# Second attention: the maxima of a pair's last four units come off in VectorE, from a broadcast tile, and not in TensorE's sum

## What is computed

```python
h = _layernorm(x, ln1_g, ln1_b)
# _attention(h, h, ...), 16 heads of 64, D_ATTN = 1024:
q = (xq @ wq).reshape(B, S, N_HEADS, D_HEAD)
...
attn = jnp.einsum('bihd,bjhd->bhij', q, k) * scale
attn = jax.nn.softmax(attn, axis=-1)
out = jnp.einsum('bhij,bjhd->bihd', attn, v).reshape(B, S, D_ATTN)
return out @ wo + bo
```

## Time and profile before

| | us |
|---|---|
| median of 3 runs | 2147.8 (2146.59 to 2148.71) |
| the profiled execution, its own time | 2148.86 |
| span of its profile | 2147.1 |
| TensorE busy in the span | 2020.2 (94%) |
| VectorE busy | 1134.3 (53%) |
| ScalarE busy | 929.5 (43%) |
| GpSimd busy | 773.0 (36%) |
| the second attention, from its first unit to its end | about 802 to 1680 |

### The profile page before, as it was taken

How to read it: one execution, slowest core, us unless ns; L and a number is a source line. 1 busy time by engine, 2 the same in 40 slices (tenths; PEclk the granted TensorE clock), 3 DMA queues, 4 the chain that set the end, 5 groups by cost and what they waited for, 6 DMA issues and landing times. The chain is left out here.

```text
span 2147.1 us, 26642 instructions
## 1 busy us (share of the span) xinstructions
PE 2020.2 (94%) x10302; PEld 1201.3 (56%) x10302; DVE 1134.3 (53%) x2025; ACT 929.5 (43%) x1441; POOL 773.0 (36%) x563
## 2 busy tenths in 40 slices
PE   5989998898998989999999999999999999999997
PEld 3544444576676754444544445444543878676776
DVE  4677772635455457756555554555454333546453
ACT  3356666333334325555445554555356431222221
POOL 1222212112223126666546664666564010212121
PEclk9999999899999989999999999999999999999999
DMA  7734332000000020200000000000000340000000
GB/s 145 137 36 52 42 57 85 1 1 1 0 1 1 1 67 1 70 1 1 1 1 1 1 1 1 1 1 1 1 1 1 97 112 1 1 10 0 10 10 10
DMA packets 48044, 51.81 MB, mean 24 GB/s; under 512 B 14682, under 2 KB 38940, under 8 KB 47620
## 3 DMA queue, kind: packets, MB, share of 16 engines
q1 hardware_dynamic: 47924, 50.19, 11.3%
HBM read 41.24 MB, written 8.80 MB: 23 GB/s over the span
## 5 line engine op out<-in xcount | busy, mean ns | idle before, releaser
L1921 POOL TENSOR_TENSOR total<-total,pr 128x1024 f32<-128x1024 f32 x183 | 444.2, 2427 | 230.9 <-ACT pr L2131 214.2
L2131 ACT ACTIVATE pr<-sc 128x1024 f32<-128x1024 f32 x256 | 259.8, 1022 | 267.0 <-PE sc L1797 262.4
L1942 DVE TENSOR_REDUCE pmax<-ring 128x1 f32<-128x512 f32 x512 | 314.5, 684 | 98.3 <-PE ring L1745 98.3
L1797 PE MATMUL sc<-q_full,k_full 64*128 64x512 f32 x1024 | 294.9, 589 | 0.0
L1815 PE MATMUL o<-pr,v_pair 128*64 128x512 f32 x1024 | 247.7, 605 | 0.0
L1745 PE MATMUL ring<-k_round,q_round 64*128 64x512 f32 x512 | 214.0, 568 | 6.0 <-DVE k_round L1936 2.0
L645 ACT ACTIVATE probs<-s 128x512 f32<-128x512 f32 (+1 forms) x304 | 154.8, 581 | 95.8 <-PE s L360 95.1
L993 POOL TENSOR_TENSOR c_scores<-c_scores,c_total 128x1024 f32<-128x1024 f32 (+1 forms) x48 | 76.5, 1615 | 237.6 <-DVE c_total L942 237.6
L483 DVE TENSOR_REDUCE row_max<-s 128x1 f32<-128x1024 f32 (+3 forms) x128 | 125.0, 1019 | 59.1 <-PE s L346 58.7
L1745 PEld LDWEIGHTS ring<-k_round,q_round 64*128 64x128 f32 x512 | 78.5, 189 | 137.6 <-DVE pmax L1942 115.5
L1797 PEld LDWEIGHTS sc<-q_full,k_full 64*128 64x128 f32 x1024 | 128.9, 191 | 25.9 <-issue 16.8
(11 more groups left out here) (349 smaller groups left out, 3425.1 us busy)
## 6 DMA issues: line engine op xcount, KB each, us to landing
qk_dram<-qk_parts SPq DMA_DIRECT2D x32, 192.0 KB, 2.7
q_stack<-qk_dram SPq DMA_DIRECT2D x48, 128.0 KB
k_stack<-qk_dram SPq DMA_DIRECT2D x48, 128.0 KB
x<-in_x SPq DMA_DIRECT2D x4, 512.0 KB, 7.4
region<-in_L_xattn_mlp_w SPq DMA_DIRECT2D x2, 1024.0 KB, 7.9
region<-in_L_xattn_ff_w SPq DMA_DIRECT2D x1, 2048.0 KB, 18.6
out<-region SPq DMA_DIRECT2D x8, 256.0 KB, 2.2
region<-in_L_xattn_sa_wo SPq DMA_DIRECT2D x1, 1024.0 KB, 8.1
```

Source lines behind the costliest of these rows:

```text
L1797: ins = te.matmul(s2[at % 2][:, j], kf[n % 2][head[j], keys], qf[n % 2][head[j], halves[half]], start=False, stop=True)
L1921: pool.tensor_tensor(out=total[half][:], in0=other[:], in1=probs[at % KEPT][:], op=ALU.add).then_inc(sums, 1)
L1942: dve.tensor_reduce(part_max[:, j, t, half:half + 1], ring[bank_of_max(i)][:], AX.X, ALU.max).then_inc(s1_free, 1)
L2131: act.activation(probs[here % KEPT][:], s2[at % 2][:], ACT.Exp).then_inc(s2_free, 1)
```

## The change

For units 12 to 15 of every pair but the last (`shifted_later`), TensorE no longer adds the maxima; the two scores' matmuls start the sum. In their place `less(n, u)` in VectorE reads the PSUM tile and adds `spread`, a tile that holds the negated maxima of half 1 in fp32 on all partitions, and writes the result to the `probs` tile; ScalarE takes the exponential in that tile, in place. The PSUM tile is free when `less` is done (`bank_free`) and not when the exponential is. `spread` is filled by two more transfers for each pair on SP's queue: `top` as a whole to DRAM, and from there, broadcast, 128 x 4 KB. Both writes to DRAM are waited for before the shift is read back; the broadcast is issued behind the shift, once the pair before has done its last `less`.

In VectorE's order `less(n, 12)` stands ahead of `split(n + 1)`, and `less(n, 13)` behind it; `less` of unit 13 stands ahead of the `late` work and the additions to `x` of that unit. Besides, the output bias is loaded into a tile that exists already (`proj_brep`), and two pairs of semaphores become one each, without other instructions.

```diff
@@ tiles and semaphores
-        wo_w, wo_brep = e.wide, sb("wo_brep", [P, C])
+        wo_w, wo_brep = e.wide, e.proj_brep
...
+        spread = sb("spread", [P, 2, 512])
...
+        spread_in, less_made = sem("spread_in"), sem("less_made")
...
+        LESS = 12
+        shifted_later = lambda n, u: u >= LESS and n + 1 < PAIRS
+        less_count = lambda n, u: (U - LESS) * n + u - LESS + 1
...
+        def buffer_free(engine, here):
+
+            if here < KEPT:
+                return
+            engine.wait_ge(pv_made, here - KEPT + 1)
+            half, kt = divmod((here - KEPT) % U, 8)
+            engine.wait_ge(sums, 7 * (2 * ((here - KEPT) // U) + half) + (kt or 1))
@@ SP
                 sp.dma_start(e.top_dram[n % 2, :, 0:16].rearrange("s r q -> r s q"), top_parts[n % 2][:]
                              ).then_inc(top_out, 16)
-                sp.wait_ge(top_out, 16 * (n + 1))
+                sp.dma_start(e.top_whole[n % 2], top[:]).then_inc(top_out, 16)
+                sp.wait_ge(top_out, 32 * (n + 1))
...
+                if n + 1 < PAIRS:
+                    if n:
+                        sp.wait_ge(less_made, less_count(n - 1, U - 1))
+                    sp.dma_start(spread[:], e.top_whole[n % 2].rearrange("(j t) q -> j (t q)", j=2)[:, 512:T]
+                                 .partition_broadcast(P)).then_inc(spread_in, 16)
@@ TensorE
+            def bank_free(at):
+                if at < 2:
+                    return
+                what, n, u = turns[at - 2]
+                if what == "unit" and shifted_later(n, u):
+                    te.wait_ge(less_made, less_count(n, u))
+                else:
+                    te.wait_ge(s2_free, at - 1)
...
-                if at >= 2:
-                    te.wait_ge(s2_free, at - 1)
+                bank_free(at)
                 keys = slice(kt * P, (kt + 1) * P)
-                for j in two:
-                    te.matmul(s2[at % 2][:, j], picks[head[j]], shift[n % 2][head[j], halves[half]], start=True,
-                              stop=False)
+                late = shifted_later(n, u)
+                if not late:
+                    for j in two:
+                        te.matmul(s2[at % 2][:, j], picks[head[j]], shift[n % 2][head[j], halves[half]], start=True,
+                                  stop=False)
                 for j in two:
                     ins = te.matmul(s2[at % 2][:, j], kf[n % 2][head[j], keys], qf[n % 2][head[j], halves[half]],
-                                    start=False, stop=True)
+                                    start=late, stop=True)
@@ VectorE
+            def less(n, u):
+                here, at = U * n + u, order_of(n, u)
+                dve.wait_ge(s2_made, at + 1)
+                dve.wait_ge(spread_in, 16 * (n + 1))
+                buffer_free(dve, here)
+                dve.tensor_tensor(out=probs[here % KEPT][:], in0=s2[at % 2][:], in1=spread[:], op=ALU.add
+                                  ).then_inc(less_made, 1)
...
                     if u == TURNED_AT - 1:
                         divide(n, 0)
+                    if shifted_later(n, u):
+                        less(n, u)
                     if u == TURNED_AT and n + 1 < PAIRS:
                         split(n + 1)
                     late(n, u)
@@ ScalarE
+                    if shifted_later(n, u):
+                        act.wait_ge(less_made, less_count(n, u))
+                        act.activation(probs[here % KEPT][:], probs[here % KEPT][:], ACT.Exp).then_inc(s2_free, 1)
```

More of the change, by code:

```diff
@@ L1638, in part_attention2 @@
         cand_less, cand_gated, mixed, power_set = (sem(n) for n in ("cand_less", "cand_gated", "mixed_late", "power_set2"))
[L1639 to L1642, removed]
+        n6_stats_made, n6_moments_made, n6_rstd_steps, n6_h_made, finished = (
+            sem(f"n6_{n}") for n in ("stats_made", "moments_made", "rstd_steps", "h_made", "finished"))
+        n7_stats_made, n7_moments_made, n7_rstd_steps, late_h_made, late_turned, late_kept = (
+            sem(f"l7_{n}") for n in ("stats_made", "moments_made", "rstd_steps", "h_made", "turned", "kept"))
         head = (slice(0, 64), slice(64, P))
@@ L1894, in _, with rstd_of @@
                 pool.tensor_tensor(out=e.xc0[s][:], in0=e.xc0[s][:], in1=e.cand0[s][:], op=ALU.add).then_inc(mixed, 1)
-            def rstd_of(count, moments, rstd, moments_made, shifted, made):
+            def rstd_of(count, moments, rstd, moments_made, steps):
                 pool.wait_ge(moments_made, 1)
                 pool.tensor_tensor(out=rstd[:], in0=moments[:, :, 1], in1=e.eps[:].to_broadcast([P, count]),
-                                   op=ALU.add).then_inc(shifted, 1)
-                pool.wait_ge(shifted, 1)
-                pool.tensor_tensor(out=rstd[:], in0=rstd[:], in1=power[:, 0:count], op=ALU.pow).then_inc(made, 1)
+                                   op=ALU.add).then_inc(steps, 1)
+                pool.wait_ge(steps, 1)
+                pool.tensor_tensor(out=rstd[:], in0=rstd[:], in1=power[:, 0:count], op=ALU.pow).then_inc(steps, 1)
             for n in range(PAIRS):
@@ L2001, in finish_chain @@
             def finish_chain():
-                dve.wait_ge(n6_rstd_made, 1)
+                dve.wait_ge(n6_rstd_steps, 2)
                 for s in two:
@@ L2028, in late @@
                 elif (n, u) == (1, 15):
-                    dve.wait_ge(n7_rstd_made, 1)
+                    dve.wait_ge(n7_rstd_steps, 2)
                     for t in range(TB):
@@ L2122, in _ @@
                     at, here = order_of(n, u), U * n + u
-                    act.wait_ge(s2_made, at + 1)
-                    if here >= KEPT:
-                        act.wait_ge(pv_made, here - KEPT + 1)
-                        half, kt = divmod((here - KEPT) % U, 8)
-                        if kt:
-                            act.wait_ge(sums, 7 * (2 * ((here - KEPT) // U) + half) + kt)
-                        else:
-                            act.wait_ge(sums, 7 * (2 * ((here - KEPT) // U) + half) + 1)
-                    act.activation(probs[here % KEPT][:], s2[at % 2][:], ACT.Exp).then_inc(s2_free, 1)
+                    if shifted_later(n, u):
+                        act.wait_ge(less_made, less_count(n, u))
+                        act.activation(probs[here % KEPT][:], probs[here % KEPT][:], ACT.Exp).then_inc(s2_free, 1)
+                    else:
+                        act.wait_ge(s2_made, at + 1)
+                        buffer_free(act, here)
+                        act.activation(probs[here % KEPT][:], s2[at % 2][:], ACT.Exp).then_inc(s2_free, 1)
                     if u == 8 + DEN_AT:
@@ L2684, in program @@
         e.top_dram = nc.dram_tensor("top_dram", [2, 3, 32, P], BF16).ap()
+        e.top_whole = nc.dram_tensor("top_whole", [2, 16, P], F32).ap()
         small = chain_loads0(nc, e, A, sb)
```

8 lines of the change are left out of this document (4 added, 4 removed).

## The result

The changed kernel takes **2164.7 us** (median of four runs, 2162.43 to 2165.02) against 2147.6 us (2146.59 to 2148.71) of the kernel before on the same chip: a ratio of 1.0074, 95% interval 1.0062 to 1.0087. It is slower by 0.7%, 17.1 us by the medians, where 16.3 were forecast. The two profiled executions are 13.6 us apart (2162.43 and 2148.86), and of the traces that is the number to explain.

What follows compares the result with a forecast made beforehand. TensorE was taken to bound the second attention (busy 870.8 of 878.0 us). Terms 4.2 + 0.1 + 4.2 + 4.25 + 2.0 + 1.6 = +16.3 us on the 2147.8 median gave 2164.1 us; own range 2156 to 2178.

Steps and rivals of the forecast that it cites:

- The new wait: Unit 15 waits 1.18 us for less(13), queued behind the split; each of eight ordinary pairs 0.52 us longer, +4.2 us.
- rival D: Some pairs go as rival B and some as the forecast: 2142 to 2160, about 2152 us; chance 0.10.
- less at 1.23 us: Each less on VectorE, 128x1024 from PSUM plus spread from SBUF, takes 1.23 us, bounds 1.1 and 1.5.
- less(12) free ahead of the split: less(12) costs the split nothing: the first cast waits for GpSimd's addition anyway, and the split ends at 1127.54 again.
- Rival B: Faster: the second cast finds GpSimd idle, takes 0.2 us, and less(13) precedes unit 15; -6.3 us, 2141.5; chance 0.13.
- rival C: Slower still: less itself holds GpSimd off, about +2.9 us at each pair's sums, some +45 us, 2193; chance 0.07.
- Unit 12 saves nothing: Unit 12's 0.22 us is not got: the transpose behind it waits for rmax, whose end hangs on GpSimd.
- 0.22 us for each of units 13 to 15: Removing the two shift matmuls saves TensorE 0.22 us per unit, 0.66 us for each pair, 9.9 us in all.
- Pairs 4, 8, 12: Second project_out behind unit 13 waits for ScalarE's v_pair copy, late behind less(13) and exp(13); +1.4 us each, +4.2.
- Pairs 0, 1 and 3: Long VectorE work between less(13) and less(14) delays GpSimd's additions and the sums' matmul: +2.0, +4.25 and +1.6 us.
- The transfers: Sending the whole maxima out on SP's queue and broadcasting spread both cost 0.
- The range: Own range of the forecast case 2156 to 2178 us; 2149 to 2178 given with the chances, leaving out rivals B and C.

Runs made afterwards that it cites:

- e3: Changed kernel with the split reading its inputs from PSUM, so no step has two SBUF inputs or is a cast from SBUF; 2143.72 us, ratio 0.998 to the kernel before.
- e6: Changed kernel with only units 14 and 15 through VectorE, units 12 and 13 taking the shift on TensorE again; 2149.43 us, ratio 1.0008.
- e5: Changed kernel with unit 12 given back to TensorE, so only units 13 to 15 go through VectorE; 2163.06 us, ratio 1.0074.
- e8b: e3 with the moments of pairs 0 and 1 moved behind less(14); 2140.73 us, ratio 0.9969 to the kernel before.
- e7: Changed kernel with the whole maxima sent out and broadcast for pair 0 only, later pairs subtracting pair 0's maxima; 2164.79 us, ratio 1.0085.
- e1: Changed kernel with less(13) moved up between the split's first cast and the subtraction behind it; 2164.86 us, ratio 1.008.
- e8: e8b with the join of the maxima (rmax) as a reduction over one input instead of a maximum of two; 2141.5 us, ratio 0.9971.

## Why the prediction was right

Point by point, by its own steps:

- **The new wait** was named at its place: TensorE idle ahead of unit 15, ended by less(13). Unit 15 was forecast 8.24 us after unit 12 and came 8.14 after it. The wait itself was forecast at 1.18 us and is 0.72 by record. By the spacing of starts it is 0.89 (units 14 and 15 start 1.85 apart, in `e3`, where nothing waits, 0.96): it is shorter because units 13 and 14 save 0.19 us less than forecast, and less(13) ended 0.10 earlier. `e6` and `e3` take that wait away in two ways, and both times the ordinary pairs become shorter than before. The eight ordinary pairs are alike (0.52 or 0.53), so rival D falls.
- **less at 1.23 us**: 1.19 to 1.226 in all 60, median 1.21:

```profile
L2005 DVE TENSOR_TENSOR pr<-sc,spread x60: 1190/1210/1226, 839.6 to 1642.7; 128x1024 f32<-128x1024 f32 x60
```

- **less(12) free ahead of the split** (`e5`): the first cast became 0.95 for 2.07 us, and ends 4.03 us after unit 12 (1131.20 less 1127.17) as it did before (4.01). A wait for the end of an addition absorbs work put ahead of it. Rival B failed by little: add(12) starts at 1131.27, 0.28 us ahead of the second cast (1131.55), and that cast took 2.26 us again. The Trainium skill (SBUF — State Buffer, "Who interferes with whom") says that a VectorE instruction with at most one SBUF input, outside its two-port modes, does not contend with GpSimd; the trace agrees: less(12) takes 1.21 us beside an addition of 2.72 (1128.40), which took 2.70 at the same place before (1121.83), and less(15) takes 1.23 beside one of 2.39. So rival C falls.
- **Unit 12 saves nothing**: unit 12 to unit 13 is 1.38 us in both kernels (1128.55 less 1127.17; 1121.99 less 1120.61), as `rmax` sets it.
- **0.22 us for each of units 13 to 15** was mis-sized. From the first matmul of unit 13 to its neighbour `values` is 1.18 us before (1123.17 less 1121.99) and 1.06 now: 0.12 saved. Units 14 and 15 together go from 2.26 (1129.28 less 1127.02) to 1.92 in `e3` (1125.15 less 1123.23): 0.12 and 0.22. The forecast took 0.22 from a unit's inside, the distance from its first shift matmul to its first scores' matmul, but the end counts. What fits the rows: the two shift matmuls covered the load of the first fp32 weights, and without them a unit that begins behind other work shows it (its four matmuls take 1.13 instead of 1.02 by record), while one right behind another unit still has it covered. That cause is read from the rows and was not tested by itself; the sizes 0.34 (`e6`) and 0.47 (`e3`) fit it. In an ordinary pair of the changed kernel the error hardly shows: unit 15 saved 0.11 less than forecast, and the wait ended 0.1 earlier. That the two cancel, and 0.52 came out to the hundredth, is luck.
- **Pairs 4, 8, 12** (forecast 1.4, measured 1.43): the copy is late and the second `project_out` waits for it. It starts 1.66 us later than before (16.64 us behind the first half's sums for 14.98) where 1.85 were forecast, and 0.23 come back behind it where 0.43 were: the chain is right, and that the sum fits so well is luck again. In pair 4:

```profile
1068.58 0.58 ACT L2135 ACTIVATE v_pair<-ring 128x512 f32<-128x512 f32 x1
...
1069.21 2.00 PE L1803 MATMUL ring<-region,aT 128*128 128x256 f32 x8 [1.63 <-ACT v_pair L2135]
```

- **Pairs 0, 1 and 3** had the right chains, each 0.4 us too long. Pair 1:

```profile
902.85 0.64 DVE L2038 BATCH_NORM_AGGREGATE l_moments<-l_stats 128x2 f32<-128x6 f32 x8
...
908.37 1.65 POOL L1933 TENSOR_TENSOR l_rstd<-l_rstd,l_power 128x8 f32<-128x8 f32 x1
...
912.47 1.08 PE L1838 MATMUL sc<-total,ones 128*64 128x512 f32 x4 [3.12 <-POOL total L1953]
```

The moments were forecast to end at 903.6 and ended at 903.49, the sums' matmul at 912.9 and came at 912.47 (the pair's transpose stands at the same time in both traces). The terms that were too large are the additions (2.35 to 2.40 us each where nothing waits, 2.49 taken) and the handing over from step to step. Only the moments' part of the chain (+2.7) is left in `e6`, and `e8b` takes nearly all of it away by order alone. In pair 3 the sums' matmul waits 1.82 us for GpSimd, which the bias addition held off, much as before (1.90); it moves by 1.22 because the bias addition, now behind less(13), starts 1.15 us later in the pair.
- **The transfers**: 0, by `e7`.
- **The range** is stated with two lower ends, 2156 and 2149; no sum stands behind the second, and D, put at 2142 to 2160, reaches below both. The measured time lies inside either.

So the expected 16.3 us were 15.2 by the distances, the difference being the 0.4 us in each of three pairs. The medians are 17.1 apart; where the other 1.9 us lie was not measured (last section).

## What to carry to other kernels

Moving work off the bounding engine pays only if the instruction that takes its place can run as early as the bank it frees is wanted: ask what stands ahead of it in its engine's queue, how much of that is waiting, and for whom. A cheap step whose length is a wait for another engine hides work put ahead of it and delays all work put behind it; shorten that step (here by its operands' memory) before something urgent is queued there, and it turned a loss of 0.7% into a gain of 0.2%, and of 0.3% with the moments moved too. And size what a removed instruction saves by the distance to the next block of work, not by the distance inside its own.

## What the runs showed of the hardware that was not expected

**After one wait for GpSimd, one more step passes.** After a VectorE step has waited for an addition's end, the next step that would have to wait takes its short time if it is issued at once: `top_rest` 0.28 us behind the first cast, the third part 0.28 behind the second, `aT` 0.68 behind `rmax`. The one after that waits again: the second cast, issued 0.03 us behind `top_rest`, took 2.26, since the next addition had begun. With 1.2 us of other work behind the first cast `top_rest` itself waits, 1.51 us (`e1`). Shortening one such step (`rmax`, `e8`) makes the next one pay (`aT`, 2.02).

**TensorE's clock fell after some waits for the sums.** In `e6` the second part of pair 1 took 30.68 us instead of 28.98, in `e1` 31.92, in `e8` that of pair 3 took 30.72. Each follows a wait of TensorE for GpSimd's sums (2.83, 3.54 and 1.82 us). The matmul of the sums in `e6`, and stretches around and behind it, in the columns of the earlier trace rows:

```profile
910.42 1.57 PE L1838 MATMUL sc<-total,ones 128*64 128x512 f32 x4 [2.83 <-POOL total L1953]
```

```profile
910.00:912.00 2.00, 1.58 (x5) 0.31 (x5) 2.00 (x2) 0.00 (x0) 2.00 (x2) 0.72 0.04 8
912.00:914.00 2.00, 2.00 (x3) 0.97 (x4) 2.00 (x6) 1.94 (x3) 0.63 (x1) 0.50 0.00 0
914.00:916.00 2.00, 2.00 (x5) 0.89 (x5) 1.60 (x5) 1.16 (x2) 0.00 (x0) 0.93 0.00 0
```

A granted clock of 0.50 is the level of 1.2 GHz; TensorE was busy throughout the second stretch. It had been idle for 2.83 us just ahead. The changed kernel waited longer at the same place (3.12 us) and kept 1.00 in its profiled execution, and pair 3's 1.82 us (1.90 before the change) had no such fall in the other kernels. So a wait of this kind costs 1.7 to 2.9 us more in some executions and nothing in others. Whether that is what raises the changed kernel's median over the sum of its distances was not measured. The record fits it: the mean granted clock of its profiled execution is 0.977, that of its other three, which took 2.2 to 2.6 us longer, 0.975 or 0.976, and in `e3` the four longest executions (2144.34 to 2144.92) have 0.975, the profiled one (2140.49) 0.977.
